# MLP bias product moved into the opening's first wait, its weights fetched with the constants, and placeholders placed anew between the opening tiles

## The reference

```
x = x + attention(_gn(x), Wq, bq, Wk, bk, Wv, bv, Wp, bp)   # 8 heads of 16 channels, 1024 tokens
x = x + mlp(_gn(x), conv_w, conv_b, ln_g, ln_b, w1, b1, w2, b2)

# attention, for each image and head
q, k, v = Wq t + bq, Wk t + bk, Wv t + bv
out = softmax(q k^T * 16**-0.5) v ;  out = Wp out + bp
# second block: 7x7 depthwise convolution + conv_b, layer norm over channels, then
y = (y - mu) * rsqrt(var + eps) * ln_g + ln_b
h = gelu(y w1 + b1)          # 128 -> 512
y = h w2 + b2                # 512 -> 128
```

## Time and profile before

| what | us |
|---|---|
| median of 3 timed runs | 314.36 |
| lowest and highest of them | 313.17, 314.5 |
| the profiled execution's own time | 311.52 |
| its span, from the first to the last instruction | 309.6 |
| TensorE busy in the span | 293.9 |
| VectorE busy | 228.6 |
| ScalarE busy | 176.6 |
| GpSimd busy | 79.4 |

### The profile page before, as it was taken

How to read it: one execution, slowest core, us unless ns; L and a number is a source line. 1 busy time by engine, 2 the same in 40 slices (tenths; PEclk the granted TensorE clock), 3 DMA queues, 4 the chain that set the end, 5 groups by cost and what they waited for, 6 DMA issues and landing times.

```text
span 309.6 us, 5462 instructions
## 1 busy us (share of the span) xinstructions
PE 293.9 (95%) x2101; PEld 134.6 (43%) x2103; DVE 228.6 (74%) x264; ACT 176.6 (57%) x354; POOL 79.4 (26%) x103
## 2 busy tenths in 40 slices
PE   7899999999999999999999999999999989999895
PEld 2535434445445444444345445444333444323342
DVE  2858444887997988989668898998997158986321
ACT  1442134887887877877768877776318645011321
POOL 7102405233200000000002878998320100101010
PEclk9998556999999999999999999999999999999999
DMA  6275000320330330231211429800000005730001
GB/s 221 35 142 94 11 0 0 55 50 6 51 54 4 50 57 10 45 52 20 34 29 26 110 66 193 179 6 1 3 0 2 0 2 135 176 121 0 0 34 34
DMA packets 8488, 16.30 MB, mean 53 GB/s; under 512 B 2564, under 2 KB 3716, under 8 KB 8464
## 3 DMA queue, kind: packets, MB, share of 16 engines
q1 hardware_dynamic: 8048, 15.29, 23.1%
q10 hardware_dynamic: 416, 0.69, 1.0%
HBM read 4.96 MB, written 1.73 MB: 22 GB/s over the span
## 4 chain that ended last, share of the span: by engine, by line
PE 78%; DVE 9%; ACT 7%; issue 2%; DMA 1%; POOL 1%; SPq 0%; DVEq 0%; ACTq 0%; POOLq 0%
PE ps L1051 20%; PE ps L1062 19%; PE ps L1152 10%; PE ps L1004 8%; ACT pr L656 7%; DVE mx L767 5%; PE ps L1210 5%; PE ps L1224 5%; PE ps L978 2%; PE ps L1041 2%; DVE ot L777 2%; PE ps L945 1%; DMA w<-wpack 1%; PE ps L1196 1%; PE ps L1168 1%
## 5 line engine op out<-in xcount | busy, mean ns | idle before, releaser
L767 DVE TENSOR_REDUCE mx<-ps 128x1 f32<-128x1024 f32 x128 | 151.1, 1220 | 39.4 <-PE ps L1004 39.4
L656 ACT ACTIVATE pr<-ps 128x512 f32<-128x512 f32 x256 | 133.3, 603 | 53.3 <-PE ps L1051 52.8
L1051 PE MATMUL ps<-qs,ks 50*128 50x512 f32 x256 | 98.1, 451 | 6.0 <-ACT pr L656 3.6
L1004 PE MATMUL ps<-ks,qs 48*128 48x512 f32 x256 | 102.2, 464 | 1.0 <-DVE mx L767 1.0
L1051 PEld LDWEIGHTS ps<-qs,ks 50*128 50x128 f32 x256 | 43.9, 189 | 60.5 <-ACT pr L656 39.8
L1062 PE MATMUL ps<-pr,va 128*32 128x256 f32 x1024 | 69.6, 389 | 0.4 <-ACT pr L656 0.4
L1004 PEld LDWEIGHTS ps<-ks,qs 48*128 48x128 f32 x256 | 44.8, 194 | 11.7 <-DVE mx L767 4.3
L1062 PEld LDWEIGHTS ps<-pr,va 128*32 128x32 f32 x1024 | 26.8, 110 | 29.9 <-ACT pr L656 11.8
L483 POOL CAST mparts<-mx 128x8 fp32r<-128x8 f32 x16 | 3.0, 190 | 134.3 <-DVE mx L767 134.3
L805 DVE SCALAR_TENSOR_TENSOR hl<-xpad,w,hl 128x512 f32<-128x512 f32 (+1 forms) x37 | 35.6, 962 | 0.9
L1152 PE MATMUL ps<-xr,wt 128*32 128x512 f32 x272 | 31.0, 594 | 0.0
(11 more groups left out here) (104 smaller groups left out, 204.9 us busy)
## 6 DMA issues: line engine op xcount, KB each, us to landing
qs<-hl SPq DMA_DIRECT2D x48, 64.0 KB, 2.4
ks<-hl SPq DMA_DIRECT2D x47, 64.0 KB, 2.4
xr<-xpad SPq DMA_DIRECT2D x16, 95.0 KB, 2.2
xr<-pad_dram SPq DMA_DIRECT2D x4, 361.0 KB, 5.9
xr<-pad_dram SPq DMA_DIRECT2D x4, 304.0 KB, 4.8
xr<-xpad SPq DMA_DIRECT2D x8, 76.0 KB, 2.1
xr<-xpad ACTq DMA_DIRECT2D x8, 76.0 KB, 2.2
xs<-x SPq DMA_DIRECT2D x2, 256.0 KB, 2.9
```

What stands on the lines that cost most here:

```text
L656: nc.scalar.activation(pr[:, n % PR, c * HALF:(c + 1) * HALF], bank("half", n, c), ACT.Exp, scale=SCALE).then_inc(exp_done, 1)
L767: nc.vector.tensor_reduce(mx[:, s % 2, i:i + 1], sm[(NT * s + i) % 2], AX.X, ALU.max).then_inc(max_done, 1)
L1004: last = nc.tensor.matmul(sm[k % 2][:, c * HALF:(c + 1) * HALF], qs[rows, cell_of(s) + i * P:cell_of(s) + (i + 1) * P], ks[rows, cell_of(s ...
L1051: nc.tensor.matmul(bank("half", n, c), ks[rows, cell_of(t) + j * P:cell_of(t) + (j + 1) * P], qs[rows, cell_of(t) + c * HALF:cell_of(t) + ...
```

## The change

The load of w1 is issued on SP right behind bv, ahead of all stacks, and has a semaphore of its own; w2 keeps its place with another. `first_bias` is called after `project_v(0, 0, NT)` and before `value_bias`. `project(1, 0)` waits for b1s as well, since it overwrites the product's bank; VectorE adds b1 right behind `bout`, ahead of all maxima. The opening has `keep_busy(3)` instead of 4 in front of tile 0, one placeholder after tile 2 where none stood, and two after every tile from 4 on that has no projection behind it (before: one after 4, 6 and 8, two after 10, 11 and 12; none after 5). `turn_max(0)` no longer waits for b1s, and the first `mlp_down` waits for w2.

```diff
@@ SP
             sp.dma_start(bv[:, :], bvrow.rearrange("a p -> p a")).then_inc(S("bv"), 16)
+            sp.dma_start(w1s[:, :], w1).then_inc(S("w1"), 16)
             for n in range(PARTS):
                 stack(sp, 0, 0, n)
...
-            sp.dma_start(w1s[:, :], w1).then_inc(S("w12"), 16)
-            sp.dma_start(w2s[:, :, :], w2.rearrange("(f p) c -> p f c", p=P)).then_inc(S("w12"), 16)
+            sp.dma_start(w2s[:, :, :], w2.rearrange("(f p) c -> p f c", p=P)).then_inc(S("w2"), 16)
@@ GpSimd
-            g.wait_ge(S("w12"), 32)
+            g.wait_ge(S("w1"), 16)
@@ VectorE
                 .then_inc(S("bout"), 1)
 
+            v.wait_ge(S("lnb"), 1)
+            nc.vector.tensor_tensor(b1s[:, :], lnb, vec(V_B1, FC), ALU.add).then_inc(S("b1"), 1)
...
                 maxima(*divmod(k, NT))
-                if k == 6:
-                    v.wait_ge(S("lnb"), 1)
-                    nc.vector.tensor_tensor(b1s[:, :], lnb, vec(V_B1, FC), ALU.add).then_inc(S("b1"), 1)
@@ TensorE
-                t_.wait_ge(S("w12"), 32)
+                t_.wait_ge(S("w1"), 16)
+                t_.wait_ge(S("gn_ve"), B)
                 for f in range(FC):
...
             project_v(0, 0, NT)
+            first_bias()
             value_bias()
+            t_.wait_ge(S("b1"), 1)
             project(1, 0)
...
-            keep_busy(4, sm[0][:, 0:HALF])
+            keep_busy(3, sm[0][:, 0:HALF])
             for k in range(AHEAD):
...
+                if k == 2:
+                    keep_busy(1, st[1])
                 if k == 4:
                     t_.wait_ge(S("copied0"), 1)
-                if k == 5:
-                    first_bias()
                 if k in (7, 9):
                     project_v(1, 2 * (k - 7), 2 * (k - 5))
                 if k == 9:
-                    t_.wait_ge(S("b1"), 1)
                     turn_max(0)
-                if k in (4, 6, 8, 10, 11, 12):
-                    keep_busy(1 + k // 10)
+                if k >= 4 and k not in (7, 9):
+                    keep_busy(2)
...
                 if f == 0:
+                    t_.wait_ge(S("w2"), 16)
```

## The result

| | us |
|---|---|
| changed kernel, median of 4 executions (301.84 to 302.53) | 302.12 |
| kernel before, median of 4 beside them (313.17 to 315.43) | 314.43 |
| ratio, 95% interval | 0.961 (0.9575 to 0.9648) |
| forecast | 303.0, range 300.5 to 308.0 |
| profiled execution after: time, span | 301.95, 300.0 |

A forecast was written before the change was run, and what follows sets the result against it. TensorE's stream bounds the kernel, slowed by a clock at 1.2 GHz from about 28 to 52 us. Terms 0.9 + 0.1 - 4.6 - 5.0 - 0.5 = -9.1 gave 302.4 profiled; with 0.6 offset 303.0, range 300.5 to 308.

The forecast's parts named there:

- loads: w1 issued on SP ahead of stacks 0 and 1, w2 and later stacks one DMA issue earlier: cost zero.
- product ahead, tile 0: MLP bias product put in front of the opening, not hidden by the stack: tile 0 from 18.16 to about 19.05, +0.9 us.
- tiles 0 to 7: Opening up to tile 8: product gone -0.98, five new placeholders +1.25, waits covered -0.2; +0.1 us (0 to +0.5).
- tiles 8 to 12: Tile 8 to the first step of head(0), at 2.4 GHz if the clock holds: 6.8 instead of 11.4 us, -4.6.
- first steps of head(0), `times_v`: Three steps of head(0) and the first times_v at full clock: 5.6 instead of 10.6 us, -5.0.
- from there to the end: The step before the clock's rise at 52.1, now at full clock: -0.5 us more.
- first `times_v` done: Sign in the profile after: first times_v done near 41.5 to 42.5 us, where it was 50.6.
- The trigger: Thin stretch at 24.7 to 28.2 us, with eight one-column instructions taking 0.98 us, makes the clock fall; 48-row tiles second reason.
- The rise: Clock's return at 52 us comes right after the first times_v, 16 dense 128-row matmuls in 1.93 us.
- Falls earlier: Rival: clock falls between the values' projection and project(1, 0), everything from about 18 us at 1.2 GHz; 321 us, chance 0.12.
- falls all the same: Rival: clock falls near where it fell before, nothing gained; 313 to 316 us, chance 0.08.
- falls late: Rival: clock holds through the middle, falls at tiles 9 to 12, half the gain there remains; 307 us, chance 0.07.

The follow-up runs named there:

- e10: Kernel before with only the load of w1 moved ahead of the stacks: 301.77, 314.17, 314.61, 314.92 us.
- e3: Changed kernel with its opening placeholders using 48 of 128 rows: 300.77, 311.18, 313.05, 317.81 us.
- e4: Changed kernel with each opening placeholder replaced by four of one column: 310.40, 310.83, 311.56, 312.31 us.
- e7: Changed kernel with the MLP bias product computed three times in a row at its new place: 305.42, 306.06, 306.13, 306.14 us.
- e2: Kernel before with only the new placeholders, bias product and load left where they were: 302.26, 315.25, 315.71, 315.72 us.
- e1: Changed kernel with the placeholders of before, so only load and MLP bias product are moved: 301.59, 302.15, 302.30, 317.53 us.
- e6: Changed kernel without the MLP bias product on TensorE (b1s is b1 alone): 301.04, 301.69, 302.62, 303.25 us.
- e8: Changed kernel with bias product and value bias between fourth and fifth tile of the values' projection: 301.65, 302.07, 303.61, 303.70 us.
- e9: The changed kernel with that product and value bias inside the values' projection, plus fewer placeholders ahead of tile 0 and in head(0): 300.84, 301.83, 301.74, 301.76 us.

## Why the prediction was right, point by point

| step | forecast | measured |
|---|---|---|
| start of the values' projection | as before, 12.91 | 12.59, 0.3 sooner by the scatter of the start |
| loads | 0 | 0.6 to 0.7 above before (e10), within the scatter of the start; not settled |
| product ahead, tile 0 | 18.16 to 19.05, +0.9 | 18.52; from the values' projection 5.25 before, 5.93 after, +0.68 |
| tiles 0 to 7 | +0.1, 10.44 from tile 0 to tile 8 | 10.23 (18.52 to 28.75) |
| tiles 8 to 12 | 6.8 | 6.64 (28.82 to 35.46) |
| first steps of head(0), `times_v` | 5.6 | 5.93 (35.46 to 41.39) |
| from there to the end | -0.5 | -0.4 (259.0 to 258.6) |
| first `times_v` done | 41.5 to 42.5 | 41.39 |
| profiled execution | 302.4 | 301.95 |
| median | 303.0 | 302.12 |

*The mechanism.* The changed kernel keeps the clock at 2.4 GHz: right, and the trace shows it. What the placeholders must be is shown by e3 and e4: made thinner by rows or by columns, they lose the clock in three and in four of four executions. *The trigger.* I named the one-column stretch as the cause and the number of rows as a second reason. Both have evidence: e10's clock falls right behind the product, e7 makes a fall with the product alone, and with placeholders of 48 rows the clock fell three times in four although the product was gone from there. So the second weighs more than I gave it. The placeholders do not do it alone (e2); whether the moved product nearly does (e1) stays open.

*The rise.* I read the rise at 52 as coming right after the first `times_v`. It came 1.4 us after its end (50.6 to 52.1), and in e4 and e10 only after a second one. The readings of the long fall's end are thus looser than the prediction has them, which did not matter, since the fall did not occur.

*The product.* The +0.9 was the product and its sum less one placeholder; that net move measured +0.68. e6's +0.89 is the product's cost with the placeholders unchanged, for which my terms give 1.13 (0.98 and 0.15), so its agreement with 0.9 is a coincidence. The stack did not end last, as I said. The SP queue has eleven DMAs of stacks 0 and 1, not ten, which changes nothing.

*The tiles.* Five new placeholders cost less than the product and the waits that went. VectorE's 1.2 us per tile (4.82 us for four maxima from 24.18 on) covers them. The first steps of `head(0)` were sized 0.3 us too low: the first matmul of each takes 0.43 us on the chain, where I took 0.24 for all four. Together the profiled execution came out 0.45 us below 302.4, of which 0.3 is the start of that execution and no merit of the sum.

*The timed median.* I left 0.6 of the 2.8 us between the profiled execution of before and its median as a fixed offset. After the change there is almost none (301.95 and 302.12). The two were apart because the stretch at 1.2 GHz is longer or shorter from one execution to the next: mean clocks of 0.962 to 0.939 with times of 312.3 to 317.25 for the same program (the profiled one, 311.52, is at 0.961). The assumption was right and could have been carried through, to 302.4.

*What I did not see.* The kernel before sometimes takes 301 to 302 us. From four executions that all fell I treated the fall as fixed. A reader of a single profile can't see this; the differing times of the runs were a hint. So "12 us faster" holds for the usual execution, and against the good one the change is by these few executions 0.4% slower.

*The rivals.* "Falls earlier" was put at 321 us. e7 lengthened the thin stretch until it came true, and it cost 1.6 us. The assumption that failed there is that the clock stays low through the opening once it has fallen; in e7 it was back after 3.4 us, as tile 0 began. As a risk to the forecast it was thus much smaller than its 10 us, though its mechanism exists. No execution of ten shows "falls all the same" or "falls late" at the price given to them; the place of the short fall in the one at 304.57 is not known.

## What to carry to other kernels

An engine that is busy in every stretch can still be starved of its clock: read the granted clock beside the busy time, and price the same instruction at both levels before believing that a stretch is bound by its work. Small matmuls (one column, few rows) should stand between dense ones, not in a stretch that is thin already; here a fall ahead of the thin stage cost 11 to 15 us, and one ahead of dense work 1.6 (e7). Where a time depends on the clock, look at a dozen executions with the mean clock of each, since a kernel can have a good case that one profile never shows.

## What the runs showed of the hardware

- The clock fell with TensorE busy 4.00 of 4.00 us (e2) and behind a stretch with 35 instructions in 4 us (e4), and held with 3.58 of 4 us busy (e1). With the product moved, full-height placeholders went without the long fall in ten of ten executions; as many of 48 rows lost the clock in three of four.
- At 1.2 GHz, a mix of tiles and full placeholders did not bring it back in 20 us. It came back 1.4 us after the first `times_v` (before), or only after the second (e4 at 53.6, e10 at 56.5), and in e7 behind `project(1, 0)` and two placeholders, 3.4 us after it fell.
- The same program falls in one execution and not in the next: 5 of 33 timed executions of the kernel before held the clock, at 301.0 to 302.3 us against 312.3 to 317.3.
- A short fall costs 1 to 1.8 us (e8: 301.65 and 302.07 against 303.61 and 303.70; e9: spans of 299.0 against 300.0), the long one in the opening 11 to 15 beside the held executions on the same chip.
